# First and third layer: 16-channel queries and keys on groups of array columns and rows, and group averages one slot later

## What is computed

```python
# layers 0 and 2: self-attention with 16-channel queries and keys
q = x @ Wq + bq; k = x @ Wk + bk; v = x @ Wv + bv      # Wq, Wk: 128 x 16
x = gamma * (softmax(q @ k.T) @ v) + x                 # 256 x 256 per image
# layer 1: 2-D Hartley transform, two block-diagonal layers with relu on each
# frequency and its partner, shrinkage, transform back, + x
# layer 3: group norm (32 groups of 4 channels), then attention with 128-channel q, k
xn = (x - mean) * rsqrt(var + 1e-6) * gn_gamma + gn_beta
x = x + (softmax(q(xn) @ k(xn).T / sqrt(128)) @ v(xn)) @ wo + bo
```

## Time and profile before

| | |
|---|---|
| Runs | 122.34 us median of 3 (122.14 to 123.2) |
| The profiled execution | 121.79 us, of which the span of the page is 120.0 us |
| PE busy | 111.1 us, 93% of the span |
| PEld busy | 100.0 us, 83% |
| DVE, ACT, POOL busy | 68.2, 64.6, 37.4 us (57%, 54%, 31%) |
| Chain that ended last | PE 79%, POOL 8%, DVE 5%, ACT 4% |
| Granted TensorE clock | 0.993 |

### The profile page before, as it was taken

How to read it: one execution, slowest core, us unless ns; L and a number is a source line. 1 busy time by engine, 2 the same in 40 slices (tenths; PEclk the granted TensorE clock), 3 DMA queues, 4 the chain that set the end, 5 groups by cost and what they waited for, 6 DMA issues and landing times.

```text
span 120.0 us, 2270 instructions
## 1 busy us (share of the span) xinstructions
PE 111.1 (93%) x728; PEld 100.0 (83%) x728; DVE 68.2 (57%) x286; ACT 64.6 (54%) x186; POOL 37.4 (31%) x97
## 2 busy tenths in 40 slices
PE   6899999999998999999989999989979799999770
PEld 5588999999998899999979998969769598999450
DVE  0126777666685666666627776666646545666511
ACT  4014666566565366664467666653546536666510
POOL 0100390000000000000023336668777786853400
PEclk9999999999999999999999999999999999999997
DMA  3899300000000000000000000000000011011211
GB/s 80 201 288 414 124 0 5 3 0 0 3 5 0 0 0 0 0 5 0 0 0 3 0 5 0 0 0 3 0 0 5 0 44 43 14 48 39 78 51 44
DMA packets 3068, 4.51 MB, mean 38 GB/s; under 512 B 480, under 2 KB 2272, under 8 KB 3056
## 3 DMA queue, kind: packets, MB, share of 16 engines
q1 hardware_dynamic: 2048, 2.59, 6.8%
q10 hardware_dynamic: 1008, 1.78, 4.5%
HBM read 3.32 MB, written 1.05 MB: 36 GB/s over the span
## 4 chain that ended last, share of the span: by engine, by line
PE 79%; POOL 8%; DVE 5%; ACT 4%; issue 2%; DVEq 0%
PE banks L547 15%; PE banks L591 10%; PE banks L539 8%; PE banks L528 7%; PE banks L565 7%; PE banks L585 6%; PE banks L652 4%; PE banks L642 3%; PE banks L643 3%; POOL probs L380 3%; PE banks L664 3%; DVE negated L874 2%; PE banks L731 2%; PE banks L606 2%; POOL rstd L415 2%
## 5 line engine op out<-in xcount | busy, mean ns | idle before, releaser
L380 POOL TENSOR_TENSOR probs<-probs,inverse 128x256 f32<-128x256 f32 x32 | 19.0, 615 | 55.3 <-DVE inverse L882 55.3
L874 DVE TENSOR_SCALAR_CACHE_REDUCE negated<-banks,v 128x256 f32<-128x256 f32 x48 | 21.4, 481 | 14.7 <-PE banks L547 14.6
L751 ACT ACTIVATE probs<-negated,lowest 128x256 f32<-128x256 f32 x48 | 23.7, 497 | 2.0 <-DVE negated L874 2.0
L742 ACT ACTIVATE u<-banks,uw 128x256 f32<-128x256 f32 x24 | 11.4, 475 | 24.6 <-PE banks L528 24.6
L759 ACT ACTIVATE probs_t<-banks 128x512 f32<-128x512 f32 x24 | 14.3, 595 | 11.5 <-PE banks L565 11.5
L591 PE MATMUL banks<-probs_t,v 128*128 128x256 f32 x64 | 17.4, 394 | 1.6 <-ACT probs_t L759 1.6
L565 PE MATMUL banks<-ident_columns,probs 128*128 128x128 f32 x96 | 14.4, 273 | 0.0
L591 PEld LDWEIGHTS banks<-probs_t,v 128*128 128x128 f32 x64 | 11.3, 190 | 3.4 <-ACT probs_t L759 2.3
L901 DVE TENSOR_TENSOR stream<-banks,stream 128x256 f32<-128x256 f32 x16 | 6.8, 425 | 10.1 <-PE banks L591 10.1
L565 PEld LDWEIGHTS banks<-ident_columns,probs 128*128 128x128 f32 x96 | 11.4, 141 | 0.2
L865 DVE TENSOR_TENSOR v<-banks,vb 128x258 f32<-128x258 f32 x24 | 10.1, 419 | 1.8 <-PE banks L539 1.8
(11 more groups left out here) (113 smaller groups left out, 210.7 us busy)
## 6 DMA issues: line engine op xcount, KB each, us to landing
out<-stream SPq DMA_DIRECT2D x7, 128.0 KB, 1.9
rows<-in_x_rows ACTq DMA_DIRECT2D x1, 768.0 KB, 10.6
xt_in<-in_x_t SPq DMA_DIRECT2D x1, 512.0 KB, 8.9
constants<-in_constants SPq DMA_DIRECT2D x1, 450.0 KB, 10.6
layer<-in_layer ACTq DMA_DIRECT2D x1, 256.5 KB, 9.1
xt_in<-in_x_t SPq DMA_DIRECT2D x2, 128.0 KB, 4.2
rows<-in_x_rows ACTq DMA_DIRECT2D x1, 256.0 KB, 5.2
xt_in<-in_x_t SPq DMA_DIRECT2D x1, 256.0 KB, 7.2
```

The costliest lines, as they stand in the source:

```text
L380: pool.tensor_tensor(probs[:, half(job), tile, :], probs[:, half(job), tile, :], inverse[:, at, tile:tile + 1].to_broadcast([TILE, TOKENS] ...
L742: nc.scalar.activation(flat(u[:, half(job)]), u_bank, ACT.Identity, bias=uw[job.layer][:, C:C + 1]).then_inc(u_ready, 1)
L751: nc.scalar.activation(probs[:, half(job), tile, :], negated[:, half(job), tile, :], ACT.Exp, bias=lowest[:, half(job), tile:tile + 1], sc ...
L874: nc.vector.tensor_scalar(negated[:, half(job), tile, :], energy_bank(job)[:, tile * TOKENS:(tile + 1) * TOKENS], v[:, job.image % 4, tile ...
```

## The change

It makes layers 0 and 2 compute q and k directly, without the folded matrix.

- `project_u` of layers 0 and 2 becomes eight products (L540): the weights are Wq or Wk padded to 32 columns (128x32), the moving side is one tile of 128 tokens. Four of them write q, four write k, each to a different group of 32 output partitions of bank 2, so that group g holds the q tile g//2 and the k tile g%2. ScalarE adds the biases in two moves of 128 columns (L782) in place of one of 256.
- `energies` of layers 0 and 2 becomes four products (L575), each over 16 rows of one 32-row group: 128 queries with 128 keys, into one bank each (banks 0, 1, 6, 7). All four banks are used by each job, so a job's `energies` waits until VectorE has read those of the job before.
- The value products lose column 129, and VectorE negates with a constant.
- `weights2` and the layer-0 preparation go away; the seven other side results move one slot earlier. Banks 6 and 7 hold energies now, so side results and group averages move to bank 2, which `project_u` and `forward_tokens` write: each waits on `side_taken`.
- Because layer 1 still uses banks 6 and 7, the first three `energies` of layer 2 wait for layer 1's `add_turned`, and `turn` gets waits too.
- The group averages go to the end of TensorE's slot, VectorE's and GpSimd's steps on them go one slot later and to the slot's start, and `sum_means` moves from GpSimd to VectorE.

```diff
-PREPARED = {1: "weights2", 2: "weights3", 3: "values3", 4: "bias3",
-            5: "mixer0", 6: "mixer1", 7: "mixer2", 8: "mixer3"}
+PREPARED = {1: "weights3", 2: "values3", 3: "bias3",
+            4: "mixer0", 5: "mixer1", 6: "mixer2", 7: "mixer3"}
+GROUP = 32
+GROUPED = C // GROUP
+        QUARTER_BANKS = [0, 1, 6, 7]
...
             def project_u(job, now):
...
+                if sides_until(now - 1):
+                    pe.wait_ge(side_taken, sides_until(now - 1))
+                source = channels_first(job)
+                if is_plain(job):
+                    for which in range(2):
+                        for group in range(GROUPED):
+                            tile = group % TILES if which else group // TILES
+                            at = group * GROUP
+                            mm = nc.tensor.matmul(
+                                u_bank[at:at + GROUP, which * TILE:(which + 1) * TILE],
+                                plain[:, job.layer // 2, which],
+                                source[:, tile * TILE:(tile + 1) * TILE], start=True, stop=True)
...
             def energies(job):
                 pe.wait_ge(u_ready, nth(job))
+                if is_plain(job):
+                    if job.layer == MIXER + 1 and job.image < DRAIN:
+
+                        pe.wait_ge(layer_done[MIXER], BATCH - 2 + job.image)
+                        pe.wait_ge(turned_ready, BATCH - 2 + job.image)
+                    if nth(job) > 1:
+                        pe.wait_ge(negated_ready, (nth(job) - 1) * TILES)
+                    for group in range(GROUPED):
+                        own = slice(group * GROUP, group * GROUP + CQ)
+                        mm = nc.tensor.matmul(banks[:, QUARTER_BANKS[group], 0:TILE],
+                                              u[own, half(job), 0, :], u[own, half(job), 1, :],
+                                              start=True, stop=True)
...
             def forward_tokens(job):
...
                     pe.wait_ge(u_ready, BATCH)
+                    pe.wait_ge(side_taken, len(PREPARED))
...
             def slot(now):
...
+                if sides_until(now) > sides_until(now - 1):
+                    pe.wait_ge(u_ready, nth(this))
+                if completed_pair(back4) is not None:
+                    group_means(completed_pair(back4))
+                if completed_pair(back5) is not None:
+                    group_variances(completed_pair(back5))
                 if now in PREPARED:
                     prepare(PREPARED[now])
...
             def move_u(job):
+                if is_plain(job):
+                    for which, name in enumerate(("bq", "bk")):
+                        move = nc.scalar.activation(
+                            u[:, half(job), which], u_bank[:, which * TILE:(which + 1) * TILE],
+                            ACT.Identity, bias=column[f"{name}{job.layer}"])
```

More of the change, by code:

```diff
@@ L453, in slot @@
                     scale_probs(back1)
-                back3 = job_at(now, 3)
-                if back3 is not None and back3.layer == NORMED - 1 \
-                        and back3.image % PAIR == PAIR - 1:
-                    sum_means(back3.image // PAIR)
             pool.memset(minus_half[:, :], -0.5).then_inc(pool_constants, 1)
@@ L707, in slot @@
                 if attends(this):
-                    project_u(this)
-                if back4 is not None and back4.layer == NORMED - 1 \
-                        and back4.image % PAIR == PAIR - 1:
-                    group_means(back4.image // PAIR)
-                if back5 is not None and back5.layer == NORMED - 1 \
-                        and back5.image % PAIR == PAIR - 1:
-                    group_variances(back5.image // PAIR)
+                    project_u(this, now)
                 if attends(back3):
```

213 lines of the change are left out of this document (117 added, 96 removed).

## The result

| | before | after |
|---|---|---|
| device time, median of 4 runs on one chip | 122.77 us (122.14 to 123.2) | 127.7 us (127.18 to 130.3) |
| ratio to before, 95% interval | | 1.039 (1.031 to 1.048): slower |
| the profiled execution: time, span | 121.79 us, 120.0 | 127.18 us, 125.4 |

What follows compares the result with a forecast made beforehand. TensorE, busy 93% of the span, was taken to bound the kernel. Terms 1.15, 6.7, 0.7, 0.4, 3.5, -3.4 and 0.4 summed to +9.5 on 121.79 us: 131.3, median 132; range 117 to 143, its own 126 to 137.

Steps and rivals of the forecast that it cites:

- -3.4 forecast: Group averages' slots: no wait for GpSimd is left and eight products of 0.22 us stay, 1.8 - 5.2 = -3.4 us.
- the wait for the banks between layers: Layer 1 into layer 2: `energies` of slots 17 to 19 wait for `add_turned`, +3.5 us in the sum.
- The two terms: Waits for VectorE to take results: +0.4 us for side results, mainly `mixer3` before `forward_tokens`, and +0.4 for group averages.
- The +0.4 for the averages' takes: `project_u` behind the averages' products waits now and then for VectorE to take the averages: +0.4 us.
- the side-by-side case: Rival for the tiled products: all groups overlap, VectorE's takes are then uncovered, some 1.4 us; 121 us, chance 0.15.
- only the second pass of one product can run beside the first of the next: Tiled products: N products take N + 1 record times, so `energies` 0.54 us and `project_u` 0.97, together 1.51.
- The lower bound of 0.65: `energies` plus `project_u` per slot if all four groups run side by side: 0.65 us, the upper end being 2.60.
- the middle: The chosen price of `energies` plus `project_u` per slot, 1.51 us, between the ends 0.65 and 2.60.
- The 6.7 us that this step made of twelve slots: Slots 3 to 7 and 17 to 23: twelve full slots, each 0.56 us longer, +6.7 us.
- the change of shape: Three changes of the array's shape in a full slot: 0.19 in, 0.07 between, 0.09 out, 0.35 us together.
- The wait for layer3: Start: TensorE waits until 11.72 us for the load that `weights3` needs; slot 3 starts +1.15 us later.
- the second case: Rival: all groups side by side, shape changes as measured, 1.00 us a slot; 121 us, no change, chance 0.15.

Runs made afterwards that it cites:

- side_mixed: The changed kernel with side results and group averages put into bank 4, where `mix_values` writes, in place of bank 2: 126.02 us, ratio 1.031.
- averages_only: The kernel before with only the group averages' part of the change (later in the slot, `sum_means` on VectorE): 118.68 us, ratio 0.989.
- averages_again: The kernel before with only the late group averages, the same kernel as averages_only, run again later: 118.84 us against 121.95 for before.

## Why the prediction was right or wrong

**Right: the direction and the range.** Slower was given 0.68, and 127.7 us lies in the range (117 to 143) and in the forecast's own (126 to 137). The change itself was 4.9 us, half of the +9.5 of the sum, and the term that made up most of that sum was wrong.

**Right: the group averages.** -3.4 forecast, -3.39 measured in slots 20 to 30 where they stand alone.

**Right: the wait for the banks between layers.** 1.1 + 1.95 + 0.9 = 3.95 us of waiting at L575 in slots 17 to 19; the list of waits has 3.9 in three waits (1.03, 2.07 and 0.83). Its way through exponentials, y_top, y and stream is the chain of after. Against before, slots 17 to 20 lost only 2.4: the first of the three waits falls ahead of them, and the slots, forecast 1.7 longer, were 0.3 shorter.

**Right in kind, too small: the takes of side results.** The two terms were 0.8 us together; with another bank 3.1 came back. For `mixer3` 0.65 was forecast, 0.77 measured. The takes in slots 4 to 7 were taken for covered by `energies`; at 0.43 in place of 0.73 it does not cover them, and they cost 0.08 a slot. The +0.4 for the averages' takes was at least 1.26, and 1.78 came back in side_mixed. The prediction had put the uncovered price at 0.1 a slot for the first, but drawn no price for the second from the side-by-side case.

**Wrong: the price of the tiled products, the largest term.** The failing step is "only the second pass of one product can run beside the first of the next". The costs are those of all four groups running their first pass together, then their second. `energies` is 2 waves, `project_u` 4; 0.22 + 0.43 = 0.65 us in place of 1.51. The lower bound of 0.65 was what the runs showed. I chose the middle from a rule on the order of records that no row showed, while disjoint groups and banks spoke for the bound. The 6.7 us that this step made of twelve slots was the largest term of the sum; by the rows of a plain slot it is -1.1.

**Wrong in size: the change of shape.** 0.35 forecast, 0.55 measured. The way in, 0.19 from the earlier trace rows, was 0.21. The change between the two narrow shapes, estimated at 0.07, was 0.14, and the way out, 0.09 in the earlier trace rows, was 0.20: 0.11 of standing and a full-width load of 0.11 that nothing hides. The two errors have opposite signs: 0.86 too much and 0.20 too little, so that a slot came out at -0.09 us in place of +0.56. Over twelve slots that is 7.8 us.

**Missing: TensorE's level at the start.** The wait for layer3 was forecast (until 11.72; it was 11.23), but no term stood for the level, which stayed at half until 17 us. Slot 3 is 2.8 us late, not 1.15, although its products cost less than forecast at full level. Some of the 2.8 may be scatter: the kernel before has its first full entry at 9.15 us in this profile, and averages_only and averages_again, with its start, reach slot 3 at 12.20 and 15.23, not 13.96.

So the second case, all groups side by side with the change of shape priced, had the mechanism, at 121 us. What kept it from being near is the size of the shape changes (0.2 x 12 = 2.4 us), the start (+2.8 at slot 3, where that case's cheaper slot 2 gave 1.15 - 0.86 = +0.3) and the uncovered takes. The forecast lay nearer to the time by luck: its error in the products stood for these. It is right in its sign and wrong in its largest term.

## What to carry to other kernels

Small products on four disjoint groups of rows or columns cost one wave for each pass here, 0.11 us, but every change of shape around them costs 0.14 to 0.21 us on a full engine. With two such steps in a 3 us slot the gain is nearly eaten (1.30 us before, 1.20 with the changes). Look first at what the new form takes from others: the banks it spreads over (3.9 us of waits, of which 1.5 came back), the loads it needs earlier (1.45 us, and 2.4 that went with the level), the bank it shares with a slow reader (3.1 us). Compare stretches and not only times, since the start of one kernel scattered by 3 us. And take an edit of two parts apart before judging it: one part of this one is worth 3.4 us alone.

## What the runs showed of the hardware that I had not expected

- The records of four 32-bit products on four groups come in fours, 7 ns apart, and the four cost two waves of 0.108 us. Doubling the products added 0.22 and 0.44 us, and with another order of the groups the eight took 0.59 in place of 0.57.
- A change of shape cost 0.21, 0.14 and 0.20 us for the three changes of a slot. By the starts of the records that is about 0.11 us of standing plus the weight load that follows.
- A gap of 1.45 us before 11.23 us went with half level until about 17 us, and the 2.1 us wait of `energies` in slot 18 with one more fall in six of the eight profiles of grouped kernels that keep them. One kernel without the gap had its first full entry at 4.2 us in one profile and at 11.83 in another. The mean granted clock of after's four runs goes with their times: 1.0 at 127.18 and 127.39 us, 0.985 at 128.01, 0.947 at 130.3. The page's row of the granted clock shows nothing of it ahead of the first entry; the lengths of the records do.
